# Waiting for the own last vector operation only where a chain goes on, fewer copies in a sort by merging, and new instruction orders

## The reference

```python
        x3 = x.reshape(b, m, c)
        corr = jnp.einsum('bmc,bnc->bmn', x3, x3) / c
        x_sort = jnp.sort(corr, axis=-1)[..., ::-1]
        ranks = jnp.round(jnp.linspace(1.0, m - 1, NB_POOLS)).astype(jnp.int32)
        return x_sort[..., ranks]
```

## Time and profile before

| | |
|---|---|
| median of 3 runs | 5244.01 us (5235.73 to 5248.09) |
| the profiled execution, its own time | 5253.13 us |
| span of its profile | 5251.3 us |
| DVE busy | 4484.3 us, 85%, 5651 instructions |
| PE busy | 3963.6 us, 75% |
| ACT busy | 3017.1 us, 57% |
| POOL busy | 930.2 us, 18% |

### The profile page before, as it was taken

How to read it: one execution, slowest core, us unless ns; L and a number is a source line. 1 busy time by engine, 2 the same in 40 slices (tenths; PEclk the granted TensorE clock), 3 DMA queues, 4 the chain that set the end, 5 groups by cost and what they waited for, 6 DMA issues and landing times.

```text
span 5251.3 us, 59990 instructions
## 1 busy us (share of the span) xinstructions
PE 3963.6 (75%) x19026; PEld 2690.2 (51%) x19026; DVE 4484.3 (85%) x5651; ACT 3017.1 (57%) x7469; POOL 930.2 (18%) x580
## 2 busy tenths in 40 slices
PE   5665628887698877888688877888688877885387
PEld 4544314754366544755357543765357544553254
DVE  0297998899989998899989998999988999999621
ACT  4544326765476635875477645865467646553363
POOL 2253002600054001610045000620036000000000
PEclk8877759999898988988899988988899888886698
DMA  4232001311122011310123001310123001000001
GB/s 131 83 100 65 16 0 55 113 35 30 36 89 83 24 38 39 115 50 23 31 84 101 24 29 42 109 58 23 30 73 109 28 25 30 27 29 14 8 22 36
DMA packets 226079, 269.70 MB, mean 51 GB/s; under 512 B 26831, under 2 KB 188506, under 8 KB 225626
## 3 DMA queue, kind: packets, MB, share of 16 engines
q0 software_dynamic: 46080, 151.03, 9.6%
q1 hardware_dynamic: 179674, 114.65, 7.5%
HBM read 242.25 MB, written 23.34 MB: 51 GB/s over the span
## 4 chain that ended last, share of the span: by engine, by line
DVE 40%; PE 29%; issue 13%; ACT 6%; DMA 5%; SPq 4%; POOL 3%; DVEq 0%; ACTq 0%; POOLq 0%
PE bank L597 6%; DMA gath<-quads,idx 4%; DVE srt_b L772 4%; DVE srt_a L772 4%; PE bank L1204 3%; DVE srt_a L815 3%; POOL gath L735 3%; SPq L502 3%; DVE srt_b L815 3%; DVE srt_a L813 2%; DVE srt_b L804 2%; PE bank L607 2%; DVE srt_a L770 2%; DVE srt_b L813 2%; DVE act L1605 2%
## 5 line engine op out<-in xcount | busy, mean ns | idle before, releaser
L735 POOL DMA_INDIRECT gath<-quads,idx x576 | 930.0, 1615 | 3123.4 <-DVE idx L706 2585.7
L597 PE MATMUL bank<-diag,gath 128*128 128x128 f32 x4608 | 640.6, 303 | 222.3 <-DMA gath<-quads,idx 217.5
L597 PEld LDWEIGHTS bank<-diag,gath 128*128 128x128 f32 x4608 | 615.5, 217 | 269.6 <-DMA gath<-quads,idx 141.9
L630 ACT ACTIVATE diag<-ident,w 128x128 f32<-128x128 f32 x2304 | 696.3, 391 | 12.0 <-DVE w L719 12.0
L1517 PE MATMUL bank<-mu_t,e2w 128*128 128x512 f32 (+1 forms) x768 | 460.5, 685 | 198.6 <-DMA e2w<-moe_w_t 168.0
L1501 PEld LDWEIGHTS bank<-e2w,act 128*128 128x128 f32 (+1 forms) x3072 | 448.1, 214 | 212.3 <-issue 167.4
L1501 PE MATMUL bank<-e2w,act 128*128 128x128 f32 (+1 forms) x3072 | 450.8, 297 | 40.4 <-DVE act L1605 40.4
L1605 DVE TENSOR_TENSOR act<-act,h_s 128x512 f32<-128x512 f32 (+1 forms) x384 | 262.2, 686 | 243.0 <-ACT h_s L1575 231.1
L1521 PE MATMUL bank<-gated_u,e2w 128*128 128x512 f32 (+1 forms) x768 | 456.8, 680 | 15.3 <-ACT h_s L1575 11.7
L1569 ACT ACTIVATE act<-bank 128x512 f32<-128x512 f32 (+1 forms) x384 | 228.2, 594 | 347.8 <-PE bank L1517 345.8
L813 DVE TENSOR_TENSOR srt_a<-srt_b 128x1920 f32<-128x1920 f32 (+5 forms) x176 | 381.5, 2167 | 4.8 <-DVE arena L1421 0.3
(11 more groups left out here) (319 smaller groups left out, 7562.1 us busy)
## 6 DMA issues: line engine op xcount, KB each, us to landing
e2w<-moe_w_t SPq DMA_DIRECT2D x256, 170.5 KB
quads<-xn_tok SPq DMA_DIRECT2D x256, 64.0 KB
e1w<-L_ffn_w SPq DMA_DIRECT2D x256, 64.0 KB, 1.9
e2w<-moe_w_t SPq DMA_DIRECT2D x256, 64.0 KB
gath<-quads,idx POOLq DMA_INDIRECT x576
e2w<-moe_w_t SPq DMA_DIRECT2D x128, 42.5 KB
x_tok<-x SPq DMA_DIRECT2D x8, 512.0 KB, 4.0
out<-tm SPq DMA_DIRECT2D x16, 256.0 KB, 2.5
```

The lines of the kernel that those rows point to most:

```text
L597: ins = T.matmul(FB[q % 2][:, k * P:(k + 1) * P], gath[:, g % 2, k, s * C:(s + 1) * C], diag[:, g % 2, 4 * k + s], start=(s == 0), stop=(s ...
L630: ins = SC.activation(diag[:, g % 2, n], ident[:], ACT.Copy, scale=w[:, n:n + 1])
L735: pool.indirect_dma_start(gath[:, g % 2, k], None, quads, bass.IndirectOffsetOnAxis(idx[:, TG * g + k:TG * g + k + 1], 0)).then_inc(sem["g ...
```

## The change

**Waits.** `Chain` gets `put` (raise the semaphore) apart from `wait`. Where a piece ended with `link(ins)`, it now ends with `link.put(ins)`, and `link.wait()` stands ahead of the stream's next piece, after its other waits. The named second raise is gone: the instruction raises `corr_used`, `g_e`, `m_ge` or `state` itself. In `stats` the third of four operations is waited for under the fourth, twice, with one `settle` more.

**The sort's copies.** Two steps make a round: the first goes from `here` to `there`, the second back. Only k/2 values next to the ends are copied in the first of them (at k = 1, the last step, the ends themselves). For m = 4 the smaller values are written in place, and 1024 values are copied back (L821, every fourth value) in place of 2048. In a half image, 22 copies become 13: gone are five of 512 values, three of 128 and one of 32. `rank_groups(k)` makes 2, 4 and 7 groups of cells for k = 4, 2, 1.

**Orders.** All strings of the early, full, late and drain bodies are new, but for SP's of the early body. The letters of each stream are as many as before, except two more S in each DVE string with a sort.

```diff
--- before.py
+++ after.py
@@ ORDER, two of its rows @@
     DVE_full=(
-        "MCSCMSSSSSSCCMMMMMSCCFMSSSSSSCFSCFMSSSFMSCCCCCSSCSMSSSSSSSSSSSSSSSSSSSSSCFFFFCFSSSSSSSMSCSSCSSSS"
...
+        "MCMSSCSSMSSMSMSSCCFFCFCMSSFMSSSMSSCSSSSSCMMSSSSCMCMCSSCMCSSSCMSSSSSSMSSSSSMSSSSMSSSSCFMFSSCFFMFS"
...
@@ rank_groups @@
-def rank_pieces():
-    pieces = []
+def rank_groups(k):
+    assert all(r // 8 == c for c, r in enumerate(RANKS))
+    groups = []
     for c, r in enumerate(RANKS):
-        if pieces and r == pieces[-1][2] + 8 * pieces[-1][1]:
-            pieces[-1][1] += 1
+        if groups and groups[-1][2] == r % 8 // k:
+            groups[-1][1] += 1
         else:
-            pieces.append([c, 1, r])
-    return pieces
+            groups.append([c, 1, r % 8 // k])
+    return groups
@@ class Chain @@
-            def inc(self, ins):
+            def put(self, ins):
                 ins.then_inc(sem[self.name], 1)
                 self.n += 1
             def wait(self):
                 self.eng.wait_ge(sem[self.name], self.first + self.n)
-            def __call__(self, ins, name=None):
-                self.inc(ins)
+            def __call__(self, ins):
+                self.put(ins)
                 self.wait()
-                if name:
-                    self.eng.sem_inc(sem[name], 1)
@@ dve_S, up to its last addition @@
-            def compare(size, src, dst, name=None):
+            def compare(size, src, dst):
                 lo, hi = src[:, :, 0:size // 2], src[:, :, size // 2:size]
                 if size == TOK:
                     hi = hi[:, :, ::-1]
                 V.tensor_tensor(dst[:, :, 0:size // 2], lo, hi, ALU.max)
                 yield
-                link(V.tensor_tensor(dst[:, :, size // 2:size], lo, hi, ALU.min), name)
-                yield
+                return V.tensor_tensor(dst[:, :, size // 2:size], lo, hi, ALU.min)
             def runs(buf, m):
                 return buf[:].rearrange("p g (b m) -> p (g b) m", m=m)
-            yield from compare(2, runs(corr, 2), runs(srt_a, 2), "corr_used")
+            ins = yield from compare(2, runs(corr, 2), runs(srt_a, 2))
+            ins.then_inc(sem["corr_used"], 1)
+            yield
             now = 0
             m = 4
             while m < TOK:
-                yield from compare(m, runs(bufs[now], m), runs(bufs[1 - now], m))
+                if m == 4:
+                    dve.wait_ge(sem["corr_used"], unit("corr_used", i, h))
+                else:
+                    link.wait()
+                ins = yield from compare(m, runs(bufs[now], m), runs(bufs[1 - now], m))
+                link.put(ins)
+                yield
                 now = 1 - now
                 here, there = runs(bufs[now], m), runs(bufs[1 - now], m)
+                def pairs(buf, k):
+                    y = buf[:, :, k:m - k].rearrange("p r (c s k) -> p r c s k", s=2, k=k)
+                    return y[:, :, :, 0], y[:, :, :, 1]
+                def edges(buf, at, k):
+                    return buf.rearrange("p r (c k) -> p r c k", k=k)[:, :, at:m // k - at:m // k - 1 - 2 * at]
+                def eighth(buf, e):
+                    return buf[:, :, e * m // 8:(e + 1) * m // 8]
                 k = m // 4
-                if m > 4:
-                    lo, hi = here[:, :, k:2 * k], here[:, :, 2 * k:3 * k]
-                    V.tensor_tensor(there[:, :, k:2 * k], lo, hi, ALU.max)
-                    yield
-                    link(V.tensor_tensor(there[:, :, 2 * k:3 * k], lo, hi, ALU.min))
-                    yield
-                    k //= 2
...
-                    yield
-                    k //= 2
                 while k >= 1:
-                    x, y = (b[:, :, k:m - k].rearrange("p r (c s k) -> p r c s k", s=2, k=k) for b in (here, there))
-                    V.tensor_tensor(y[:, :, :, 0], x[:, :, :, 0], x[:, :, :, 1], ALU.max)
-                    yield
-                    V.tensor_tensor(y[:, :, :, 1], x[:, :, :, 0], x[:, :, :, 1], ALU.min)
-                    x, y = (b.rearrange("p r (c k) -> p r c k", k=k)[:, :, ::m // k - 1] for b in (here, there))
-                    link(V.tensor_copy(y, x))
-                    yield
-                    now = 1 - now
-                    here, there = there, here
-                    k //= 2
+                    lo, hi = pairs(here, k)
+                    out_lo, out_hi = pairs(there, k)
+                    link.wait()
+                    V.tensor_tensor(out_lo, lo, hi, ALU.max)
+                    yield
+                    if m == 4:
+                        link.put(V.tensor_tensor(hi, lo, hi, ALU.min))
+                        yield
+                        link.wait()
+                        link.put(V.tensor_copy(lo, out_lo))
+                        yield
+                        break
+                    if k == 1:
+                        V.tensor_copy(edges(there, 0, 1), edges(here, 0, 1))
+                    elif k < m // 4:
+                        V.tensor_copy(edges(there, 1, k // 2), edges(here, 1, k // 2))
+                    link.put(V.tensor_tensor(out_hi, lo, hi, ALU.min))
+                    yield
+                    if k == 1:
+                        now = 1 - now
+                        break
+                    link.wait()
+                    if k == m // 4:
+                        for e, a, b in ((1, here, there), (3, there, there), (5, there, here)):
...
+                        link.put(ins)
+                        yield
+                    else:
+                        lo, hi = pairs(there, k // 2)
+                        out_lo, out_hi = pairs(here, k // 2)
+                        V.tensor_tensor(out_lo, lo, hi, ALU.max)
+                        yield
+                        link.put(V.tensor_tensor(out_hi, lo, hi, ALU.min))
+                        yield
+                    k //= 4
                 m *= 2
             k = TOK
             while k >= 16:
-                yield from compare(k, runs(bufs[now], k), runs(bufs[1 - now], k))
+                link.wait()
+                ins = yield from compare(k, runs(bufs[now], k), runs(bufs[1 - now], k))
+                link.put(ins)
+                yield
                 now = 1 - now
                 k //= 2
             src, stage = bufs[now], 1 - now
             for k in (4, 2, 1):
                 dst = bufs[stage % 2]
-                last = k == 1
-                for c, cnt, r in rank_pieces():
-                    base_r = r // (2 * k) * (2 * k)
-                    side = ALU.max if (r % (2 * k)) < k else ALU.min
-                    lo = cell8(src, base_r, cnt, k)
-                    hi = cell8(src, base_r + k, cnt, k)
-                    if last:
-                        out = dst[:, :, c:c + cnt].unsqueeze(3)
-                    else:
-                        out = cell8(dst, r // k * k, cnt, k)
+                link.wait()
+                for c, cnt, n in rank_groups(k):
+                    side = ALU.max if n % 2 == 0 else ALU.min
+                    lo = cell8(src, c, cnt, n // 2 * 2 * k, k)
+                    hi = cell8(src, c, cnt, n // 2 * 2 * k + k, k)
+                    out = cell8(dst, c, cnt, n * k, k) if k > 1 else dst[:, :, c:c + cnt].unsqueeze(3)
                     ins = V.tensor_tensor(out, lo, hi, side)
-                link(ins)
+                link.put(ins)
...
@@ stats @@
         def stats(dve, link, src, st, m, name):
             for t in range(UT):
+                if t == UT - 1:
+                    link.put(ins)
                 ins = V.bn_stats(st[:, t], src[:, t])
-            link(ins)
+            link.wait()
             settle(dve)
+            link.put(ins)
             for t in range(UT):
+                if t == UT - 1:
+                    link.wait()
+                    settle(dve)
                 ins = V.bn_aggr(m[:, t], st[:, t:t + 1])
             ins.then_inc(sem[name], 1)
@@ dve_route, its first pieces @@
             link(V.tensor_reduce(rows[:, 0], logits, AX.X, ALU.max))
-            link(V.tensor_tensor(gl[:], logits, ex8(0), ALU.subtract), name_e)
-            yield
+            V.tensor_tensor(gl[:], logits, ex8(0), ALU.subtract).then_inc(sem[name_e], 1)
+            yield
+            dve.wait_ge(sem[name_e], unit(name_e, i, h))
             link(V.scalar_tensor_tensor(gv[:], gl[:], 0.0, revb, ALU.is_equal, ALU.mult))
             link(V.tensor_reduce(rows[:, 1], gv[:], AX.X, ALU.max))
-            link(V.tensor_tensor(oh[:], gv[:], ex8(1), ALU.is_equal))
-            yield
+            link.put(V.tensor_tensor(oh[:], gv[:], ex8(1), ALU.is_equal))
...
```

156 lines of the change are left out of this document (85 added, 71 removed).

## The result

The changed kernel takes **5023.3 us** (5019.2 to 5026.4), the kernel before beside it 5246.1; ratio **0.958** [0.956, 0.960]. The profiled execution took 5026.4 us, with a span of 5024.6.

What follows compares the result with a forecast made beforehand. The prediction took the DVE as the bound outside the drain; waits 97, raises 14, copies 39 and rank steps 9 us sum to 159 us saved, giving 5085 us against a 5244.0 median, with an 8-in-10 range of 5040 to 5165 us.

Steps and rivals of the forecast that it cites:

- The bound: Whole run but the drain: everything queues behind the DVE, 93% busy in a full body, for some 4690 of 5251 us.
- The orders: New engine orders: earlier gathers and weights offset M's operations queued behind gathers; 42 us DVE idle per full body stay.
- Waits no longer paid and raises: DVE: 882 own waits covered by another stream's instruction, at 0.11 us, save 97 us; separate semaphore raises gone save 14 us.
- Copies and ranks: DVE sort: fewer and smaller copies save 39 us; rank steps cut from 21 to 13 operations per half image save 9 us.
- Nothing for ACT's loads: ACT: 80 more table loads, 18 us per full body, costed at nothing because ACT has slack; 103 us without that cover.
- Nothing for the drain: The 331 us drain, with no sort and 79 us of DVE work: no gain counted.
- The sign by the busy time: DVE busy time falling by less than 120 us would show the price of a wait or of strided copies wrong.
- Rival D: The new orders also remove 8 us of DVE waits per full body, 48 us more gained: 5037 us; chance 0.07.
- A: DVE is freed but PE and ACT don't follow; half of 21 us per full body lost: 5163 us; chance 0.17.
- C: Slower: gathers strewn through PE's in-order queue hold back what the DVE's M and C pieces need: 5298 us; chance 0.07.
- B: An own wait on the DVE costs nothing recoverable; only operations count, 48 us saved: 5196 us; chance 0.03.
- E: The orders still put the own successor behind almost every piece; 48 + 14 us saved: 5182 us; chance 0.02.

Runs made afterwards that it cites:

- e2: The changed kernel's waits and sort under the orders of the kernel before (one S more per sort): 5241.1 us, ratio 0.998.
- e7: The kernel before with two of F's three indirect gathers per group: 5147.4 us, ratio 0.980.
- e12: The changed kernel's waits and sort in the old orders, with two of F's three gathers per group: 5092.4 us, ratio 0.969.
- e9: The changed kernel with two of F's three gathers per group: 4952.2 us, ratio 0.942.
- e1: The changed kernel with every wait on an own operation put back at once behind that operation: 5093.9 us, ratio 0.970.
- e10: The changed kernel with the sort copies of the kernel before put back: 5021.9 us, ratio 0.955.
- e11: The changed kernel with the rank groups of the kernel before put back: 5024.6 us, ratio 0.957.
- e8: The kernel before without the 352 copies at the ends of the sort's steps: 5208.0 us, ratio 0.992.
- e16: The new orders alone: the changed kernel with waits at once, copies and rank groups of the kernel before: 5116.1 us, ratio 0.975.
- e4: The changed kernel with a tiny Exp before every second expert's SiLU, 59 table loads more: 5053.0 us, ratio 0.962.
- e14: The changed waits and sort in old orders, two of three gathers, M's weights loaded for the first two experts only: 5049.6 us, ratio 0.961.
- e3: The changed kernel with old orders and every wait at once, only its sort kept: 5262.2 us, ratio 1.002.
- e5: The kernel before with three of the four matmuls per gathered tap of F: 5237.1 us, ratio 0.997.
- e15: The changed kernel with M's weights loaded for the first two experts of a half image alone: 4955.0 us, ratio 0.944.

## Why the prediction missed

Two edits met, and the first, of waits and sort, is worth little without the second, the orders (medians; 5246 is the one beside the changed kernel):

| | before's waits, copies, ranks | the change's |
|---|---|---|
| old orders | 5246 | 5241 |
| new orders | 5116 | 5023 |

Waits, copies and ranks are worth 6 us in the old orders and 93 in the new ones; the orders are worth 136 us alone and 218 on top of the rest.

*Step by step.* **The bound** ("for some 4690 of 5251 us everything queues behind the DVE") is wrong, and it is the root. e2 shows it: some 106 us less of DVE work by the account, 6 us less time. What held the old full body, in large part, was F's chain of gather and matmul in the stretch in which PE, strictly in order, had C's and M's matmuls behind it (e7: 107 us, and the waits for `h_s` from 9.9 to 1.9; e12: the DVE's waits for M and C from 27.5 to 3.8 us). A 93% busy DVE hid it, because its idle time showed as a few scattered waits for `h_s` and L1450, whose own cause lay two steps further back. I read them as what ended the wait, not as where the wait came from, and PE's 217.5 us for gathers stood beside them.

**The orders** ("I take the two as equal: the 42 us of idle time per full body stay") is the term that was mis-sized: 0 forecast, 136 us alone and 218 beside the rest (e2 to the changed kernel). Compared with e2, a full body loses 32.4 us: 24.0 of waiting for others and 8.5 of own waits, the latter since the new orders part the pieces of a chain more often (1285 waits at once, 1762 in e2). The part that goes by the gathers, as far as thinning them by a third shows it, is the 13.7 us by which one gather is worth less now (18.6 against 4.9). With one gather away in both, 9.7 us of waiting are left between e12 and e9, and the wait for `td` at L908, 10.1 us in e12 and 0.9 in the changed kernel, is as large as that; that the orders' move of F's second norm ended it was argued, not tried.

**Waits no longer paid and raises**, 97 + 14 us: own waits fell by 120 us, so the price was right: the median wait takes 0.115 us in the traces. The smaller term was sized too low. Of gaps of 0.20 to 0.26 us, where a raise or a register instruction of the DVE's sequencer stands beside the wait, the trace before has 277 and the one after 27; 250 of them at 0.12 us more than a bare wait are 31 us, where 14 were taken for raises. The rival price of a wait from the Trainium skill's page "VectorE: DVE Perf Modes", section "The DRAIN you can't avoid", nothing for a semaphore, is not what these runs show: e1 puts 743 waits back and loses 71 us. **Copies and ranks**, 39 + 9 us: operations fell by 47 us, also right. But no share of them reached the time in the changed kernel (e10, e11), about half did in the kernel before (e8), and some 22 of 50 us behind e1 (e16).

**Nothing for ACT's loads**: the cover was probably not whole (e4, 20 to 30 us for 59 loads, with intervals that touch). **Nothing for the drain**: 4 us, as forecast.

**The sign by the busy time** misleads. The forecast called the price of a wait wrong if the DVE's busy time fell by less than 120 us; it fell by 109, and the price was right all the same. "The profile counts it as busy time" holds for 0.08 us of a wait only.

So the sum of the work was near (167 us for 159), but not its worth in time, 6 us in the old orders and 93 in the new ones; that 5085 us came as near to 5023 as it did, with nothing for the orders, is chance. The forecast's inner range was loose as well: its bounds, added up, give 5031 to 5129 us and not 5050 to 5125; neither holds 5023. *Rival D* had the right direction, and its 8 us per full body are just what the account shows (26.9 to 18.9), but it was given 0.07 and priced on top of a work term that D's own mechanism makes possible in the first place. With it, 8 us more of work and 10 us of idle time in the early and late bodies make the time. *A* and *C* fall: waiting for others went down. *B* falls with e1, and *E* with the own waits of 34.8 and 18.2 us.

What stays open: why 115 us of own waits cost 71 us in the new orders while 34 us of copies cost none. Idle time left over is a part of it: it fell to 11.4 us per full body in e1 and 13.0 in e10, so both ate into the same 18.9, and behind e1 some half of the next 50 us came through (e16). But e1's full body still had more idle time than e16's, so no clean threshold was reached; that waits stand in the chains that PE waits for, and copies at the ends of sort levels, was not tried by itself. Also open is what else the old orders lose: with one gather less and most of M's loads gone a full body still takes 583.0 us (e14), against 563.8 in e9.

## What to carry to other kernels

A busy share of 93% does not make an engine the bound when it takes its work from a queue in order: follow its few waits back through the other engines to the first late transfer, and take a piece off that (here one gather of three) before any sum of the busy engine's costs is made. An edit that shortens an engine's work and one that reorders the work are to be tried separately and together; here 6 and 136 us made 223. And a wait that the trace lists in every body (20 us for M's weights) may be worth nothing there, while the same loads cost some 43 us in the drain.

## What the runs showed of the hardware

An own wait costs the same from start to start in the kernel before, the changed one, e1, e2, e3 and e16: 0.115 us at the median, as 2.32 against 2.21 us. The copy of 1024 values, every fourth of its buffer, took 1146 ns at the median. Less the fixed 0.16 us of the forecast that is about 1.0 ns a value, where single values of another copy cost 0.9 and dense ones 0.5.

The granted clock differed with the order of the work. With the same 19026 matmuls PE was busy 3963.6 us before, 3965.3 in e2, 3817.8 in e16 and 3798.3 in the changed kernel; stretches at the lower level, 1.2 GHz, were 214 before, 202 in e2, 146 in e16 and 136 after, and lasted 1488, 1478, 1445 and 1363 us in all. PE's idle time per full body was nearly the same, 114 and 111 us. In the changed kernel 46 us of it lie together in the last 69 of the body, where the granted share is 0.69 and PE has 98 matmuls; before, 20 us did, at 0.83. The last 70 us of a full body, before and then changed:

```profile
2485.00:2554.90 69.90, 49.94 (x196) 30.86 (x194) 66.41 (x63) 22.20 (x42) 0.00 (x0) 0.83 0.12 35
```
```profile
2371.00:2440.30 69.30, 22.84 (x98) 15.09 (x97) 65.60 (x56) 12.82 (x29) 0.00 (x0) 0.69 0.00 1
```

How much of the time this clock is worth by itself no run here shows. In the old orders e5 points to little: it took 123 us off PE's busy time and gained 17. In the drain of e15 it goes with 15.6 us less of PE's busy time.

A table load of 1283 ns is followed by its activation within 0.02 us where the activation waits for nothing else. Timeline of the changed kernel, ACT:

```profile
2225.76 1.28 ACT L1621 ACT_TABLE_LOAD   x1
2227.05 0.60 ACT L1621 ACTIVATE act<-bank 128x512 f32<-128x512 f32 x1
```
